# A loop body of two iterations in the attention part of a perceiver layer

## The reference

```python
x = x + xattn(layernorm(x), ctx)      # q = x Wq, k = ctx Wk, v = ctx Wv; softmax(q k^T / 8) v Wo + bo
x = x + wkv_mix(layernorm(x), ...)    # time mixing over the 32 tokens with exponential decay per head
x = x + moe_ffn(layernorm(x), ...)    # 8 experts of 128 -> 512 -> 128, one per token by argmax
```

## Time and profile before

| what | value |
|---|---|
| median of 3 runs | 988.71 us |
| profiled execution: its own time | 989.46 us |
| profiled execution: span from the first to the last instruction | 987.7 us |
| DVE, ACT, POOL busy in the span | 80%, 68%, 80% |
| granted TensorE clock, mean over the span | 0.934 |

### The profile page before, as it was taken

The page is one execution under the profiler, slowest core; times in us unless marked ns, Lnnn a source line. Parts: engine busy times, 40 slices in busy tenths (PEclk is TensorE's granted clock), DMA queues, the critical chain, the costliest instruction groups (busy, mean ns, idle before and its releaser), DMA issues.

```text
span 987.7 us, 28200 instructions
## 1 busy us (share of the span) xinstructions
PE 847.2 (86%) x8428; PEld 704.6 (71%) x8428; DVE 788.7 (80%) x2025; ACT 673.8 (68%) x1927; POOL 791.3 (80%) x1226
## 2 busy tenths in 40 slices
PE   7989998999999999999999999999998454018883
PEld 7777787878788878888788888888876243007773
DVE  5899879898989989898989898998988566216762
ACT  3878777878777878787788878778875124008772
POOL 5788888988989898989898898989895601754885
PEclk9999999999999999999999999999999755559997
DMA  9111111111111111111111111111100670121220
GB/s 242 35 33 34 35 34 34 34 49 44 40 32 33 32 32 32 32 32 32 32 32 42 52 36 32 32 32 32 32 2 1 120 198 4 49 68 50 63 60 13
DMA packets 58286, 45.86 MB, mean 46 GB/s; under 512 B 8286, under 2 KB 56033, under 8 KB 58224
## 3 DMA queue, kind: packets, MB, share of 16 engines
q1 hardware_dynamic: 55728, 40.82, 16.9%
q0 software_dynamic: 2496, 4.26, 1.3%
HBM read 37.65 MB, written 8.32 MB: 47 GB/s over the span
## 4 chain that ended last, share of the span: by engine, by line
POOL 39%; PE 33%; issue 15%; DVE 7%; ACT 3%; POOLq 1%; DMA 0%; DVEq 0%; ACTq 0%
POOL Pn L945 13%; PE bank L381 6%; PE bank L432 5%; PE bank L403 4%; POOL cT L936 3%; POOL out_dram L1266 3%; PE bank L425 3%; PE bank L393 3%; POOL chi L926 3%; POOL sorted_rows L1248 3%; PE bank L409 2%; POOL e12p L952 2%; POOL clo L930 2%; POOL e12p L955 1%; PE bank L1363 1%
## 5 line engine op out<-in xcount | busy, mean ns | idle before, releaser
L727 ACT ACTIVATE Pe<-bank,nmax 128x257 f32<-128x257 f32 x512 | 240.9, 471 | 105.4 <-DVE nmax L790 85.6
L945 POOL TENSOR_TENSOR Pn<-Pe,rsum 128x1028 f32<-128x1028 f32 x128 | 243.0, 1898 | 41.5 <-DVE rsum L814 35.8
L381 PE MATMUL bank<-cT,qh 96*128 96x257 f16 x1024 | 184.5, 274 | 4.4 <-ACT Pe L727 2.7
L794 DVE TENSOR_TENSOR Tl<-bank,Th 128x1024 f16<-128x1024 f32 x128 | 155.4, 1214 | 2.9 <-ACT Th L716 2.9
L432 PE MATMUL bank<-identf,Pn 128*128 128x128 f32 x1024 | 149.3, 274 | 0.0
L716 ACT ACTIVATE Th<-bank 128x512 f16<-128x512 f32 x256 | 141.1, 594 | 8.9 <-PE bank L432 8.5
L381 PE MATMUL bank<-cT,ql 96*128 96x257 f16 x512 | 139.1, 272 | 0.0
L381 PEld LDWEIGHTS bank<-cT,qh 96*128 96x128 f16 x1024 | 97.5, 97 | 44.3 <-issue 8.3
L432 PEld LDWEIGHTS bank<-identf,Pn 128*128 128x128 f32 x1024 | 114.5, 141 | 6.0
L790 DVE TENSOR_REDUCE nmax<-bank 128x2 f32<-128x514 f32 x128 | 88.2, 689 | 36.4 <-PE bank L381 34.9
L803 DVE TENSOR_REDUCE nmax<-bank 128x1 f32<-128x257 f32 x256 | 105.0, 411 | 0.0
(11 more groups left out here) (214 smaller groups left out, 2388.3 us busy)
## 6 DMA issues: line engine op xcount, KB each, us to landing
rawT<-in_dram SPq DMA_DIRECT2D x32, 385.5 KB, 3.9
raw<-in_dram SPq DMA_DIRECT2D x32, 384.0 KB, 4.4
sorted_rows<-fill SPq DMA_DIRECT2D x1, 3013.0 KB, 23.9
xs<-sorted_rows SPq DMA_DIRECT2D x23, 131.0 KB, 2.2
R<-in_dram SPq DMA_DIRECT2D x4, 512.0 KB, 5.8
Z<-last_rows SPq DMA_DIRECT2D x128, 2.2 KB
w1r<-in_dram SPq DMA_DIRECT2D x4, 512.0 KB, 13.6
w2fr<-in_dram SPq DMA_DIRECT2D x4, 512.0 KB, 13.3
```

The source lines that it names most:

```text
L381: last = nc.tensor.matmul(bank[SB[t]][:, 0:M], w[:, par, b, t * P:(t + 1) * P], cT[:, s4, c, 0:M], start=(k == 0), stop=(k == 2))
L727: nc.scalar.activation(Pe[:, n_par(j + 1), t, :], bank[SB[t]][:, 0:M], ACT.Exp, bias=nmax[:, n_par(j + 1), t:t + 1], accum_out=sums[:, n_p ...
L794: nc.vector.tensor_tensor(Tl[:, n_par(j - 1), :, :], psum[:, 4:4 + MC, :], Th[:, n_par(j - 1), :, :], ALU.subtract).then_inc(s_Tl, 1)
L945: nc.gpsimd.tensor_tensor(Pn[:, par, :, :], Pe[:, par, :, :], rsum[:, par, :].unsqueeze(2).broadcast_to([P, QT, M]), ALU.mult)\
```

## The change

Iteration 4 is written out too, and the loop runs over 5, 7, 9, 11 and 13 with two iterations in its body. All four engines use the same function.

```diff
         def pipeline(eng, step):
-            for i in range(4):
+            for i in range(5):
                 for j in range(-1, 7):
                     step(i, j)
-            with eng.Fori(4, LIT - 1) as it:
+            with eng.Fori(5, LIT - 2, 2) as it:
                 for j in range(-1, 7):
                     step(it, j)
+                for j in range(-1, 7):
+                    step(it + 1, j)
             for j in range(-1, 7):
                 step(LIT - 1, j)
```

## The result

The changed kernel takes 1005.74 us (median of 5 runs, 1005.65 to 1006.28) against 988.71 us: 17.0 us slower, ratio 1.017, 95% interval 1.0156 to 1.0184. The direction was right, and so was the mechanism as far as it was forecast, code that is fetched again after each jump. The size was not: 4.0 us were forecast, and the time lies outside the range of 987.0 to 1000.0 us.

The account below looks back on a forecast made before the run. No engine alone was taken to bound the attention part, whose chain POOL and PE share. Four jumps at 1.0 us of visible fetch, other terms 0, added 4.0 us to 988.71 us: 992.7 us, range 987.0 to 1000.0 us.

Parts of the forecast that it names:

- Fewer jumps, a round written out, arithmetic on it + 1: Loop on all engines: six jumps fewer, round 4 written out, doubled register arithmetic; each taken as 0.
- A body twice as long isn't kept: Loop jumps: the doubled body must be fetched again at each of four jumps, costing 4.0 us; chance 0.50.
- What a fetch costs, 2.7 us: PE at each jump: 1.6 us transfer start plus 1.1 us packet; 1.04 us covered by transposes, 1.7 us idle.
- A second fetch behind the first: PE at a jump landing near a packet's end: two fetches, 5.4 us at most, up to 14.7 us for four jumps.
- PE makes up 0.69 us at L466: Step after each jump: PE waits 0.69 us for POOL's e12p anyway, which absorbs that much of its stall.
- 1.0 us remains: PE at each jump: 1.7 us idle less 0.7 us made up at L466; four jumps cost 4.0 us.
- The far end of the sum, 1003.4 us: Jumps: two fetches in a row, or an engine bringing in its whole window, up to 14.7 us slower; chance 0.10.
- Kept: Rival, loop jumps: all of the longer body is kept or its fetch wholly covered, no change, 988.7 us; chance 0.27.
- Collision gone: Rival, first step of a round: DVE's den, num, denm miss POOL's e12p, 4 x 0.63 = 2.5 us faster, 986.2 us; chance 0.13.
- Two fetches in a row: Rival, each jump: two fetches, or a whole window brought in, up to 14.7 us slower, 1003.4 us; chance 0.10.
- What would show it: Signs: 74 and 61 packets on q8 and q14, 2.6 us PE gap at jumps, L466 wait gone after, rounds in pairs.
- e12p: POOL operation in a round's first step: 1.19 us beside DVE's den, num and denm, 0.26 us in another round.

Follow-up runs that it names:

- the written-out kernel: Kernel before with all 16 iterations written out, no loop and no jump: 991.35 us, ratio 1.0026.
- The padding: Changed kernel with already met waits added at the program start, 57 instructions on PE and 12 on ACT: 1010.29 us, ratio 1.0214.
- the two versions that went after it: Kernel before with DVE's den, num and denm moved to the end of step 0: 1018.4 us; or with DVE waiting for e12p ahead of den: 993.15 us.
- the kernel that had no long round: Kernel before with the loop body doubled on POOL alone: 988.87 us, ratio 0.9999.
- body of four: Changed kernel with four iterations in the body on all engines and seven written out ahead, one jump: 993.99 us, ratio 1.0049.
- without a jump: Kernel with all 16 iterations written out, plus 72 met waits on PE at the heads of rounds 7, 9, 11 and 13: 1000.62 us, ratio 1.0129.
- with two jumps: Changed kernel, body of two, with nine iterations written out ahead of the loop: 998.46 us, ratio 1.0101.

## Why the prediction was wrong

**Fewer jumps, a round written out, arithmetic on it + 1: nothing.** Right as far as it was tried. Jumps to code that is kept are hidden in the earlier trace rows, POOL's doubled loop costs nothing, and the loop's own inner turn takes 0.87 us.

**A body twice as long isn't kept.** Right. Forecast for that case were 74 packets on q8 and 61 on q14; it is 81 and 76. The forecast counted 8 packets a jump for PE; (81 - 42) / 4 = 9.75 came. The stretch of 139 us in the earlier trace rows is not all ahead of the loop, since the loop's first round opens at 213.80 us. The size stands all the same: 37 packets in 445 us of the written-out kernel make 3.8 packets, 63 KB, a round of 45.9 us.

**What a fetch costs, 2.7 us.** Too small, and not by much: the turn takes 3.35 us where the transposes cover 1.04, so PE's idle is 9.5 / 4 = 2.4 us a jump and not 1.7. By the DMA view the packet on q8 starts 0.5 us after the first of the transposes and takes about 1 us, and PE goes on 2.8 to 3.0 us after that start. So the packet's own time of 1.1 us was right, but most of the wait lies behind the packet and not ahead of it, where the small loads of the earlier trace rows had put 1.6 us; what fills it no view shows.

**A second fetch behind the first.** It stood in the far end and in a rival with 0.10. By the packets it came at all four jumps, and it shows as idle at three, for 2.1 us together, 0.5 us a jump. The padding took it away, so it hangs on where the jump's target lies in the code.

**PE makes up 0.69 us at L466.** Right: 3.2 / 4 = 0.8 us, and the four waits that are gone are those of the step after each jump.

**The term that was not there.** With the sizes above a jump would cost 2.4 + 0.5 - 0.8 = 2.1 us, 8.4 us for four. The other half is the granted clock, 9.2 / 4 = 2.3 us a jump. The step that failed is the one from 1.7 us of PE idle to "1.0 us remains", by which PE idle at the turn is worth its own length less the wait behind it. Its price is twice that here, since TensorE goes on at 1.2 GHz for 3.4 or 6.8 us after it. Nothing in the loop before shows a clock of under 1.00, and no row there has PE idle for over 1.11 us; so the loop could not give the size. But it could have told me that a longer idle was outside of what it shows; the clock row of that page, shown above, stands at half in four slices behind the attention part, where PE is busy half of the time or less; and the end of the range, built from fetches alone, had no room for it. The far end of the sum, 1003.4 us, was passed for the same reason.

**The rivals.** Kept: excluded by the queues. Collision gone: the wait at L466 did fall, the two versions that went after it lost 28.9 and 3.4 us by their ratios, and the kernel that had no long round came out at a ratio of 0.9999; the supposed price of 0.63 us a round was the difference of two steps, not a time that the whole loop returns. Two fetches in a row: part of the truth; the second came, and PE's work from the first covered most of its wait.

**What would show it.** The gap at the jump was forecast at 2.6 us and is 3.35; the wait at L466 is gone in the step after each jump, as forecast, and stays in the six other rounds. Rounds do differ by whether they end in a jump: from one first score matmul of PE to the next, those that do last 48.2 to 48.4 us, 2 us more than the others with 46.1 to 46.5, though after a slow stretch of 6.8 us the next round is long too, 48.3 and 48.6 us.

## What to carry over

Before a loop body is lengthened, compare the code of one body on each engine with what the instruction queues bring during the loop: no packets means that it is kept. That says nothing of a longer body, so try each engine by itself: here PE's body made the whole loss, ACT's and DVE's a third of it when PE's was left alone, and POOL's none. Jumps to kept code and code that runs straight on showed no stall of PE here; a jump to code that is not kept is the dear one. When an edit makes TensorE idle for some us, price the clock after the gap as well as the gap.

## What the runs showed of the hardware

- One PE body of 65 KB by the queues stays on the chip, and one of twice that does not: 1 packet and 46 in the loop. The Trainium skill (Runtime: NRT & Kernel Launch, Instruction fetch mechanics) gives PE 128 KiB, and says that a jump outside the window waits for a DMA. The trace agrees with both, with 2.4 us of idle at such a jump. No run here is fine enough to place the bound.
- A jump that has to fetch stalled DVE, ACT and PE by similar times, 2.1, 1.7 and 2.4 us of idle with bodies of two, though the packets of the first two are half the size. Single stalls reached 3.7 us on PE (padded kernel) and 4.3 us on DVE (body of four).
- The same doubled body of ACT was waited for at each jump from one start in the code, and at none from a start twelve instructions further on: 76 and 55 packets on q14.
- TensorE's clock fell to half for 3.4 us behind idle of 2.5 to 2.75 us without a jump, in two cases of four, in one of them with no transfer under way; behind the jumps of the changed kernel in four of four, with PE alone doubled in four of four, with two jumps in one of two, with one jump in one, and in the padded kernel in three of four. In the kernel before, with PE never idle for over 1.11 us in the loop, it did not fall there.
- Operations of DVE and of POOL held each other up from either side: e12p 1.19 us in place of 0.26, den 2.75 us in place of 0.47.
- A wait that is already met is not free: 28 such instructions, two waits in each, made PE stand 1.75 us, and 8 more added 0.9 us.
